# First layer of a two-layer kernel: weight tiles of the shared expert in fewer transfers and one step ahead, expert rows fetched by SyncE, feature halves added by GpSimd

## What is computed

```python
xn = layernorm(x)
x = x + attn(xn) + moe(xn)

def attn(x):                      # gated linear attention, then a gated MLP
    h = rmsnorm(x, norm1_w)
    x = x + gla(h)                # 8 heads, chunks of 64
    h2 = rmsnorm(x, ffn_norm_w)
    return x + (silu(h2 @ w_gate) * (h2 @ w_up)) @ w_down      # 704 hidden

def moe(x):                       # 14 experts, 2 per token, and a shared one
    combine = top2_weights(x)
    y = sum_e combine_e * expert_e(x)                          # 176 hidden each
    return y + (silu(x @ sg.T) * (x @ su.T)) @ sd.T            # shared, 352 hidden
```

## Time and profile before

| | us |
|---|---|
| median of 3 runs | 3299.9 (3296.22 to 3306.58) |
| the profiled execution, its own time | 3303.34 |
| its span | 3301.5 |
| first layer without its experts | 24 to 884 |
| beats 1, 2, 3 and 4 begin at | 80, 172, 284, 374 |
| beats 5 to 9 begin at | 464, 552, 644, 734, 824 |

### The profile page before, as it was taken

How to read it: one execution, slowest core, us unless ns; L and a number is a source line. 1 busy time by engine, 2 the same in 40 slices (tenths; PEclk the granted TensorE clock), 3 DMA queues, 4 the chain that set the end, 5 groups by cost and what they waited for, 6 DMA issues and landing times. The chain is left out here.

```text
span 3301.5 us, 55891 instructions
## 1 busy us (share of the span) xinstructions
PE 2795.4 (85%) x16828; PEld 2069.3 (63%) x16828; DVE 2206.1 (67%) x5096; ACT 2003.2 (61%) x4382; POOL 1819.9 (55%) x1461
## 2 busy tenths in 40 slices
PE   4669999997579566658739999999999999999998
PEld 2446666665379444447627777777777777777775
DVE  3346666665366367645438888888778888888876
ACT  3335444542255354445438888888888788878886
POOL 1121111116400233432048989889898989989887
PEclk7679998998789776679769999999999999999999
DMA  5234544545743643365566666576766666666563
GB/s 135 64 112 167 178 152 141 180 158 188 228 129 124 225 130 99 120 206 173 153 199 198 186 184 197 175 207 178 215 182 188 190 184 198 183 186 196 171 197 108
DMA packets 310536, 559.87 MB, mean 170 GB/s; under 512 B 47990, under 2 KB 158966, under 8 KB 309750
## 3 DMA queue, kind: packets, MB, share of 16 engines
q1 hardware_dynamic: 296422, 518.52, 51.6%
q0 software_dynamic: 13824, 37.77, 3.6%
HBM read 439.50 MB, written 120.90 MB: 170 GB/s over the span
## 5 line engine op out<-in xcount | busy, mean ns | idle before, releaser
L2546 POOL TENSOR_TENSOR mm<-mt,cb 128x1024 f32<-128x1024 f32 x192 | 463.1, 2412 | 166.5 <-ACT mt L2505 166.5
L2488 ACT ACTIVATE mt<-a_wide,a_tok 128x128 f32<-128x128 f32 x1536 | 485.6, 388 | 6.6 <-POOL mm L2546 6.6
L2632 DVE SCALAR_TENSOR_TENSOR cv<-bank,taps,cv 128x509 f32<-128x509 f32 (+2 forms) x576 | 429.2, 745 | 13.6
L2423 PE MATMUL bank<-yz,wo 128*128 128x512 f32 x768 | 361.8, 594 | 0.0
L59 PE MATMUL bank<-f,wi 128*128 128x512 f32 x768 | 321.2, 418 | 14.1 <-DMA wi<-ssm_wi_split 14.1
L60 PE MATMUL bank<-f,wi 128*128 128x512 f32 x768 | 304.7, 397 | 0.0
L61 PE MATMUL bank<-f,wi 128*128 128x512 f32 x768 | 304.5, 396 | 0.0
L2567 POOL TENSOR_TENSOR yz<-y,zs 128x512 f32<-128x512 f32 x192 | 245.4, 1278 | 15.1
L2563 POOL TENSOR_TENSOR y<-t 128x512 f32<-128x512 f32 x192 | 245.2, 1277 | 2.2 <-DVE t L2679 2.2
L890 POOL TENSOR_TENSOR l_s_out<-l_s_raw,l_s_out 128x512 fp32r<-128x512 f32 (+1 forms) x33 | 48.7, 1476 | 343.7 <-DVE l_s_out L1137 227.5
L2577 POOL TENSOR_TENSOR y<-y,ys 128x512 f32<-128x512 f32 x184 | 234.2, 1273 | 5.0 <-ACT ys L2501 4.7
(11 more groups left out here) (443 smaller groups left out, 7488.6 us busy)
## 6 DMA issues: line engine op xcount, KB each, us to landing
wi<-ssm_wi_split SPq DMA_DIRECT2D x192, 512.0 KB
a_wide<-a_scratch SPq DMA_DIRECT2D x192, 512.0 KB, 6.0
l_fw<-ffn_split SPq DMA_DIRECT2D x72, 768.0 KB, 5.7
ea<-ea_scratch SPq DMA_DIRECT2D x384, 128.0 KB, 3.2
wo<-ssm_wo_scaled SPq DMA_DIRECT2D x192, 128.0 KB, 3.1
ssm_wi_split<-l_s_out SPq DMA_DIRECT2D x24, 512.0 KB
sorted_scratch<-fr_zeros SPq DMA_DIRECT2D x4, 3072.0 KB, 24.0
ey_x<-sorted_scratch SPq DMA_DIRECT2D x96, 128.0 KB, 2.3
```

What stands on the lines that cost most here:

```text
L2423: i = pe.matmul(bank[:, OUT + m, :], wo[:, g % R, m * P:(m + 1) * P], yz[:, g % 2], start=t == 0, stop=t == LAST)
L2488: i = act.activation(mt[:, h, chunk(j)], a_wide[:, g % R, h, chunk(j)], ACT.Relu, bias=a_tok[:, s * NJ + j, 2 * t + h:2 * t + h + 1], scal ...
L2546: pl.tensor_tensor(mm[:], mt[:], cb[:, s * NJ:(s + 1) * NJ, :].rearrange("p j t -> p (j t)") .unsqueeze(1).broadcast_to([P, 2, TS]), ALU.m ...
L2632: dve.scalar_tensor_tensor(cv[:, a:TS], bank[:, X, 0:TS - a], taps[:, t, k:k + 1], cv[:, a:TS], ALU.mult, ALU.add).then_inc(ph["tap"], 1)
```

## The change

- Splits move one place forward: n = 4k + i + 1, so split 0 runs in beat -1, the shared tiles are places 1, 2 and 3 of beat 1, and beat 8 has none. fetch(0) goes out ahead of the loop, and `keep(n)` issues `fetch(n + 1)` ahead of writing n.
- A shared tile takes 4 transfers with all its parts (128 x parts x 16 numbers) and one for each part's 16 rows; the third also two that fill the rest with zeros from SBUF, in the place of VectorE's clear. That is 12 transfers for each of the three, for 40, 40 and 30 before.
- GpSimd adds the two halves of x, of the squares and of y's squares (128 x 512 each) into the first half; mean, variance and second_square are one matmul each. For y of the last slice the two matmuls stay.
- `rows_back`: SyncE fetches the expert rows, 8 transfers of 512 rows, into the tiles h, xc, sq and x; GpSimd only scatters.
- SyncE keeps split (k,0) ahead of its wait for `x_tok`. In beats 8 and 9 the finished sum is written behind t = 2, not ahead of the hidden weights.

```diff
         def split_of(k, i):
-            n = k * PER + i
-            return n if 0 <= k and n < SPLITS else None
+            n = k * PER + i + 1
+            return n if 0 <= n < SPLITS else None
...
                 def fetch(n):
-                    if n is None:
-                        return
                     done(sp, "low", n - 1)
...
-                        if len(parts_of(n - NF)) < 8:
-                            done(sp, "s_zero", 0)
-                        for r, i in enumerate(parts_of(n - NF)):
-                            for q in range(2 * KD):
-                                sp.dma_start(s_raw[:, q * P + r * 16:q * P + r * 16 + 16],
-                                             moe0[i, :, q * P + 8 * E0:(q + 1) * P]).then_inc(ph["s_raw"], 16)
+                        parts = parts_of(n - NF)
+                        R = len(parts)
+                        tiles = moe0[parts[0]:parts[0] + R]
+                        for q in range(2 * KD):
+                            sp.dma_start(s_raw[:, q * P:q * P + R * 16].rearrange("p (r c) -> p r c", r=R),
+                                         tiles[:, :, q * P + 8 * E0:(q + 1) * P].rearrange("r p c -> p r c")).then_inc(ph["s_raw"], 16)
+                        for r in range(R):
                             sp.dma_start(s_raw[r * 16:r * 16 + 16, 2 * KD * P:MLP],
-                                         moe0[i, 8 * E0:P, 2 * KD * P:MLP]).then_inc(ph["s_raw"], 16)
+                                         tiles[r, 8 * E0:P, 2 * KD * P:MLP]).then_inc(ph["s_raw"], 16)
+                        if R < 8:
+                            w = P - R * 16
+                            sp.dma_start(s_raw[:, 0:2 * KD * P].rearrange("p (q c) -> p q c", q=2 * KD)[:, :, R * 16:P],
+                                         zeros[:, 0:2 * KD * w].rearrange("p (q c) -> p q c", q=2 * KD)).then_inc(ph["s_raw"], 16)
+                            sp.dma_start(s_raw[R * 16:P, 2 * KD * P:MLP], zeros[R * 16:P, :]).then_inc(ph["s_raw"], 16)
...
                 def keep(n):
...
                     done(sp, "low", n)
+                    if n + 1 < SPLITS:
+                        fetch(n + 1)
...
+                def kept_sum(g):
+                    bb, ts = at(g)
+                    done(sp, "evac", g)
+                    sp.dma_start(acc_dram[bb, :, :, ts], base[:, g % 3]).then_inc(ph[f"kept{g % 3}"], 16)
+
+                def rows_back(i):
+
+                    if i == 0:
+                        done(sp, "rows", G - 1, 16)
+                        done(sp, "rank_ps", G - 1)
+                        done(sp, "h_hi", G - 1)
+                        done(sp, "h_lo", G - 1)
+                    else:
+                        done(sp, "placed", 0, PLACE_OPS)
+                    if i >= RX:
+                        sp.wait_ge(swdge[f"put{i % RX}"], i // RX * 2 * RX * 16)
+                    sp.dma_start(group[i % RX], rows_dram[i * RX * P:(i + 1) * RX * P].rearrange("(r p) d -> p r d", p=P))\
+                        .then_inc(swdge[f"group{i % RX}"], 16)
+
+                fetch(0)
                 for k in BEATS:
                     a, c, f = k, k - 1, k - 2
-                    fetch(split_of(k, 0))
-                    if has(k - 3):
-                        bb, ts = at(k - 3)
-                        done(sp, "evac", k - 3)
-                        sp.dma_start(acc_dram[bb, :, :, ts], base[:, (k - 3) % 3]).then_inc(ph[f"kept{k % 3}"], 16)
+                    if has(k - 3) and has(a):
+                        kept_sum(k - 3)
                     if has(a):
                         clear(a)
+                        keep(split_of(k, 0))
                         done(sp, "x_tok", a)
...
                     else:
+                        if a == G:
+                            rows_back(0)
                         for t in range(NT):
                             hidden_weights(f, t)
...
+                            if t in (2, 4, 8):
+                                keep(split_of(k, t // 2 if t < 8 else 3))
+                            if a == G and t == 2:
+                                for i in range(1, RX):
+                                    rows_back(i)
+                            if has(k - 3) and not has(a) and t == 2:
+                                kept_sum(k - 3)
+                            if a == G and t in (4, 6, 8):
+                                rows_back(RX + t // 2 - 2)
+                            if a == G + 1 and t == 2:
+                                rows_back(2 * RX - 1)
...
                 def mean(a):
-                    pe.wait_ge(ph["x"], a * 16)
+                    done(pe, "x_half", a)
                     done(pe, "qe", a - 1)
-                    for k in range(KD):
-                        i = pe.matmul(bank[:, 2, :], col("mean"), x[:, k, :], start=k == 0, stop=k == KD - 1)
-                    i.then_inc(ph["mean"], 1)
+                    pe.matmul(bank[:, 2, :], col("mean"), sq[:, 0, :], start=True, stop=True).then_inc(ph["mean"], 1)
...
                     if has(a):
                         for n in range(0, 4):
                             masked(a, n)
+                    if has(a + 1):
+                        pl.wait_ge(ph["x"], (a + 1) * 16)
+                        done(pl, "var", a)
+                        pl.tensor_tensor(sq[:, 0, :], x[:, 0, :], x[:, 1, :], ALU.add).then_inc(ph["x_half"], 1)
                     low(split_of(k, 2))
+                    if has(a + 1):
+                        done(pl, "sq", a + 1)
+                        pl.tensor_tensor(sq[:, 0, :], sq[:, 0, :], sq[:, 1, :], ALU.add).then_inc(ph["sq_half"], 1)
+                    if has(c) and c < G - 1:
+                        done(pl, "sqy", c)
+                        pl.tensor_tensor(xo[:, 0, :], xo[:, 0, :], xo[:, 1, :], ALU.add).then_inc(ph["sqy_half"], 1)
                     low(split_of(k, 3))
                     if k in (G, G + 1):
                         n = NG // 2
-                        for i in range(min(RX, n)):
-                            fetch_rows((k - G) * n + i)
                         for i in range(n):
                             scatter((k - G) * n + i)
-                            if i >= 2 and i - 2 + RX < n:
-                                fetch_rows((k - G) * n + i - 2 + RX)
```

More of the change, by code:

```diff
@@ L294, in layer0 @@
         qb = sb("qb", [P, 4, H0, CH])
-        group = h[:].rearrange("p k t -> p (k t)").rearrange("p (r d) -> p r d", d=D)
+        group = [t[:].rearrange("p k t -> p (k t)").rearrange("p (r d) -> p r d", d=D) for t in (h, xc, sq, x)]
         RX = 4
@@ L348, in split_in @@
             shared = min(max(0, n + 1 - NF), NX)
-            eng.wait_ge(ph["s_raw"], 16 * (n + 1 - shared) + 16 * sum(5 * len(parts_of(i)) for i in range(shared)))
+            parts = [len(parts_of(i)) for i in range(shared)]
+            eng.wait_ge(ph["s_raw"], 16 * (n + 1 - shared) + 16 * sum(2 * KD + r + 2 * (r < 8) for r in parts))
         def parts_of(i):
@@ L426, in _ @@
                             .then_inc(ph["rows"], 16)
-                    keep(split_of(k, 0))
-                    fetch(split_of(k, 1))
                     if has(a + 1) and a >= 0:
@@ L433, in _ @@
                     if not has(f):
-                        keep(split_of(k, 1))
-                        fetch(split_of(k, 2))
-                        keep(split_of(k, 2))
-                        fetch(split_of(k, 3))
-                        keep(split_of(k, 3))
-                    else:
+                        for i in range(1, PER):
+                            keep(split_of(k, i))
+                    else:
+                        if a == G:
+                            rows_back(0)
                         for t in range(NT):
@@ L620, in mean @@
                 def mean(a):
-                    pe.wait_ge(ph["x"], a * 16)
+                    done(pe, "x_half", a)
                     done(pe, "qe", a - 1)
-                    for k in range(KD):
-                        i = pe.matmul(bank[:, 2, :], col("mean"), x[:, k, :], start=k == 0, stop=k == KD - 1)
-                    i.then_inc(ph["mean"], 1)
+                    pe.matmul(bank[:, 2, :], col("mean"), sq[:, 0, :], start=True, stop=True).then_inc(ph["mean"], 1)
                 def variance(a):
-                    done(pe, "sq", a)
-                    for k in range(KD):
-                        i = pe.matmul(bank[:, 2, :], col("mean"), sq[:, k, :], start=k == 0, stop=k == KD - 1)
-                    i.then_inc(ph["var"], 1)
+                    done(pe, "sq_half", a)
+                    pe.matmul(bank[:, 2, :], col("mean"), sq[:, 0, :], start=True, stop=True).then_inc(ph["var"], 1)
                 def second_square(c):
-                    done(pe, "sqy", c)
                     done(pe, "kl", min(c + 1, G - 1))
-                    for k in range(KD):
-                        i = pe.matmul(bank[:, 3, :], col("mean"), xo[:, k, :], start=k == 0, stop=k == KD - 1)
```

(20 more changed lines are left out.)

18 lines of the change are left out of this document (3 added, 15 removed).

## The result

The changed kernel takes 3249.0 us (median of four runs, 3244.1 to 3252.2), the kernel before beside it 3301.8 us: a ratio of 0.9837, 95% interval 0.9814 to 0.9859. The profiled execution has a span of 3248.5 us against 3301.5, so 53.0 us are gone. All of them, and 1.1 us more, come out of the first layer: it ends (first transfer of the experts' weights) at 829.8 us instead of 883.9.

What follows compares the result with a forecast made beforehand. TensorE was taken to bound full beats, with gaps to win only in the first layer (24 to 884 us). 12.1 + 17.9 + 9.9 + 8.6 = 48.5 us off 3299.9 gave 3251 us, range 3232 to 3271.

Steps and rivals of the forecast that it cites:

- start of beat 2 (beats 0 and 1): Beats 0 and 1: fewer transfers of shared tiles on SyncE let the last high part start sooner, 12.1 us won.
- beat 2, with its share of the norms (1.8): Beat 2: GpSimd no longer blocked, TensorE's 16.35 us wait and 1.53 us slower restart gone; halved norms besides.
- beats 3 to 7, norms: Beats 3 to 7: their 8.1 us of the 9.9 us (5 to 13.8) forecast from halving norm matmuls.
- beats 8 and 9: Beats 8 and 9: late write of the sum removes the 8.10 us weight wait and slow restart, 8.6 us won.
- The bound of 14.7 us: Beats 0 and 1, good end: ScalarE reaches its last high part at 150.4 us, so at most 14.7 us won.
- The rival of the renamed wait: Beat 2: split 9 holds GpSimd for another reason, so the wait stays; 3269 us, chance 0.04.
- The gross term of 0.86 us: Full beats: each norm on two passes instead of four saves 0.86 us, 16 times, 13.8 us in all.
- The deduction of 0.77 us per beat for VectorE: Full beats: one GpSimd addition per beat slows VectorE on TensorE's path by 0.77 us, 3.9 us over five.
- The pieces: Rival, shared tiles: 64-byte pieces, not the issue, are the limit, beats 0 and 1 win nothing; 3263.5 us, chance 0.07.
- Late additions: Rival, norms: TensorE waits for GpSimd's additions as long as it saves; 3261.3 us, chance 0.08.
- The slower one: Rival, beats 8 and 9: scatters at 3 us delay weights and the layer's end; 3326 us, chance 0.03.
- signs of being wrong: Wide transfers over 2 us each; TensorE waiting for GpSimd before lines 620 to 637; beat 8 weights landing after 5.7 us.

Runs made afterwards that it cites:

- b_wide: Kernel before with only one edit, shared tiles fetched in few wide transfers (12, 12 and 10 instead of 40, 40 and 30): 3279.4 us, 0.9931.
- u_narrow: Changed kernel with its shared tiles fetched in 16-column transfers again (40, 40 and 32 instead of 12 each): 3266.5 us, 0.9898.
- u_shift: Changed kernel with the old numbering of the splits (4k + i), shared tile 8 again first in beat 2: 3241.1 us, 0.9820.
- u_kept: Changed kernel with the write of the slice's sum back ahead of the hidden weights in beats 8 and 9: 3255.4 us, 0.9854.
- rows_shift: Changed kernel with expert rows fetched by GpSimd in 32 transfers again and the old numbering of the splits: 3248.6 us, 0.9837.
- slow_scatter: Changed kernel with one more GpSimd addition, into an unread tile, ahead of each of its 64 scatters: 3325.7 us beside 3357.8, 0.9902.
- u_rows: Changed kernel with the expert rows fetched by GpSimd in 32 transfers between the scatters again: 3295.2 us beside 3357.5, 0.9826.

## Why the prediction was right, and where its steps were off

**Sum and sign.** 48.5 us were forecast, 52.8 were measured between the medians; the traces have 54.1 us in the first layer. The terms miss by +5.8, +2.0, +0.4 and -2.6 us, so a part of the misses cancels: that much is luck. Where each came from:

| | forecast | measured |
|---|---|---|
| start of beat 2 (beats 0 and 1) | 12.1 (6 to 14.7) | 17.9 |
| beat 2, with its share of the norms (1.8) | 17.9 + 1.8 | 21.7 |
| beats 3 to 7, norms | 8.1 | 8.5 |
| beats 8 and 9 | 8.6 (4 to 12.6) | 6.0 |

**Beats 0 and 1.** The mechanism held: b_wide and u_narrow show it from both sides. The size was off, by 5.8 us, past the good end. Three terms: GpSimd's `masked` came at 129.61 us where the sum took 132.92, 47.1 us into the beat and not 52.5, with TensorE at 2.4 GHz from 87 to 92 us and in parts around it (0.67 granted over the first 25 us of beat 1), where the kernel before spent them all at 1.2 GHz (0.50; shown below); split 7's write landed 3.0 us after its issue ended, where 5.7 was taken from a load of the same size; and the 1.0 us for a longer beat 0 can't be read: the beat is 1.9 us longer in this pair, but five traces without additions have it between 42.7 and 45.9 us. The bound of 14.7 us was wrong in kind: it took ScalarE's arrival, 150.4 us, as fixed, and that moves with the beat. Five us near the start of beat 1, first of the changed kernel, then of the kernel before (the clock is the third number from the end):

```profile
87.00:92.00 5.00, 5.00 (x46) 2.67 (x45) 3.21 (x7) 1.53 (x3) 2.05 (x2) 1.00 0.00 2
```

```profile
90.00:95.00 5.00, 5.00 (x28) 2.39 (x24) 3.73 (x11) 2.33 (x4) 1.56 (x2) 0.50 0.00 0
```

**Beat 2.** The wait of 16.35 us went, and the 1.53 us of the slower restart too: from the scores at 179.23 us to the outputs at 183.82 us it is 4.59 us, as in beat 4. The step that failed is the reason given, that split 9 stands in split 8's place. u_shift leaves split 8 there and has no wait. Of the 16.35 us, 9.5 go with 20 fewer issues and the other 6.9 with the clear, which held the fetch until the middle of the beat, and with fetching ahead. The rival of the renamed wait rested on the same belief, that the order of splits decides.

**Norms.** The gross term of 0.86 us for each two passes was right: 2.8 us per beat in the means of nine traces and four, for beats 3 to 6. In the changed kernel a mean is now 1.02 us for two passes. The deduction of 0.77 us per beat for VectorE was wrong in who pays it. The collision is there: in each of beats 2 to 6 VectorE's scaled part (line 1158, 1137 before) takes 1.38 us beside the addition of x, where it took 0.34, so VectorE loses 1.04 us per beat. Beat 4, line 1140 and what follows it, then the same of the kernel before:

```profile
382.57 1.47 DVE L1140 TENSOR_TENSOR l_u_lo<-l_su,l_u_hi 128x512 fp32r<-128x512 f32 x1 [0.70 <-ACT l_u_hi L771]
383.96 1.38 DVE L1158 TENSOR_SCALAR l_s_out<-l_s_raw 128x256 f32<-128x256 f32 x1
```

```profile
424.83 0.34 DVE L1137 TENSOR_SCALAR l_s_out<-l_s_raw 128x256 f32<-128x256 f32 x1
```

Line 1140 is long beside `masked`, as before; the addition of x runs from 383.45 to 385.19 us, under line 1158. But TensorE has no wait there that it didn't have before (one, of 0.52 us, in both traces), and in all of beats 3 to 6 it waits 17.1 us for `su`, 14.8 before. So the forecast of 8.1 us for beats 3 to 7 met 8.5 in the pair of traces with a wrong term in it. By the means it is 4 x 2.8 + 0.9 = 12.1 us for these beats, and a single trace lies up to 6 us beside its mean; what beats 0 to 2 take back leaves 7.3 us, under the forecast of 9.9 for all norms.

**Beats 8 and 9.** The wait of 8.10 us is gone, and u_kept brings it back as 8.40. From beat 8's start to its first hidden tile it is 42.9 us, 37.3 before: TensorE waits 13.6 us for `place` instead of 12.0, since `masked` 6 and 7 now run beside it (with the old numbering they stand behind a low part, and the wait is 12.0 again in u_shift and rows_shift), and then it stays at 1.2 GHz from 706 to about 729 us. That takes back most of what shorter waits for weights (4.3 us to land instead of 5.7, over the layer) give. The 6.0 us is the difference of one pair: b_wide, with the code of the kernel before, takes 154.8 us for these beats, 5 more than that kernel, while the late write alone costs 7.6 us by u_kept.

**Rivals.** The pieces: out by the 0.54 to 0.64 us per issue. Late additions: no wait for them in a full beat. The slower one, scatters that hold the end: slow_scatter shows the mechanism as a real one, but in part. With scatters from 706.3 us on, the layer's end follows GpSimd from (829.8 - 3.4 - 706.3)/64 = 1.9 us per scatter, and the sign would change at (883.9 - 3.4 - 706.3)/64 = 2.7 us. Both are means with the pauses in them: the changed kernel has 1.5 us, slow_scatter 2.4. 2.6 was forecast, but from a start at 752.5 us, 46 us too late, which the sum forgot to move with the rest of the layer. The rival's own price doesn't add up either: 944 us is 60 us after the end at 884, not 66. The weights are not held.

**Signs.** Beat 2 starts at 154.1 us (160 forecast), beat 3 at 243.2 (252; before it began at 282.8 us, not at the 284 of the table, so beat 2 took 110.7 us and not 112), full beats take 87.1 to 89.7 us (87.5), the layer ends at 829.8 (835), beat 9 starts without a wait, and the last scatter starts at 802.97 us, 21 us ahead of the last matmul (30). Two of the signs of being wrong show in part: TensorE waits for the additions in beats 0 and 1, and of the five weight loads of beats 8 and 9 whose landing the trace shows two took 7.0 and 6.6 us (issued at 768.7 and 782.7 us), but no wait for weights there is over 1.6 us.

## What to carry to other kernels

A tile gathered from many small pieces costs the queue that issues it, not the DMA engines, as long as their share in that stretch is low (0.19 here): count issues times 0.48 us first. A wait that ends on an engine's own in-order work is best followed to the first thing that work waited for: here a clear of 0.70 us, not the order of the tasks, kept a fetch back for half a beat. On TensorE's path halving the passes paid in full where every beat was full (2.8 us per beat for three norms, beats 3 to 6), with the additions on an engine whose own work is not on that path; over all beats it was 7.3 us, so read such a price over the whole stretch that the edit touches.

## What the runs showed of the hardware

- Full beats of one and the same code take 85.3 or 89 us. The difference lies in the attention part. Ten us after the start of beat 3 the changed kernel's TensorE stays at half clock for two stretches of five us and part of a third, that of u_rows for part of one, with TensorE busy throughout and the same single wait of 2.1 us before it. Four us per beat are decided there, more than the norms win. Changed kernel, then u_rows:

```profile
253.20:258.20 5.00, 5.00 (x29) 2.16 (x30) 4.45 (x9) 2.68 (x4) 2.57 (x3) 0.50 0.28 92
258.20:263.20 5.00, 5.00 (x36) 2.53 (x38) 2.20 (x5) 0.00 (x0) 3.27 (x3) 0.50 0.22 20
```

```profile
253.01:258.01 5.00, 4.99 (x39) 2.18 (x38) 4.82 (x10) 2.69 (x4) 2.56 (x3) 0.66 0.27 92
258.01:263.01 5.00, 5.00 (x58) 3.15 (x58) 4.49 (x8) 1.27 (x2) 3.57 (x3) 1.00 0.24 50
```

- In two of the experiments' four jobs the kernel before took 3357 us instead of 3303, and in those GpSimd's unbroken rows of indirect DMAs went with a standstill of the other engines: VectorE's idle time of 35 to 39 us in the first layer, in all four traces that had such a row there, and TensorE busy 11 to 12 instead of 30 to 32 us beside the second layer's row, in all six. With a row transfer or an addition of GpSimd between the first layer's scatters there was none in that layer, in two kernels. What VectorE waits for there the trace doesn't say (it names no engine of the core, or the issue). The changed kernel itself wasn't run in such a job; since all ten such rows (four and six) were held, it is likely to be held in the first layer too, with a smaller gain: the four have 0.991 to 0.997, u_rows 0.983. That makes the rows on GpSimd the safer choice of two that are equal elsewhere. What sets such a job apart isn't known: the same chip number stands at one of either kind.
